# A window-attention, MLP and channel-attention kernel: MLP and channel attention put into one program

## What is computed

```python
# block 0: windows of 8 x 8 shifted by 4, attention over 12 heads, then an MLP over channels
xn = _layernorm(x, norm1_g, norm1_b)
attn = softmax(q @ k.T * scale + bias + mask)
x = shortcut + roll(attn @ v @ proj_w + proj_b)
h = _layernorm(x, norm2_g, norm2_b)
h = gelu(h @ fc1_w + fc1_b)
x = x + (h @ fc2_w + fc2_b)
# block 1: channel attention; mean and variance are of a whole image
mu = mean(x, axis=(1, 2, 3)); var = mean((x - mu) ** 2, axis=(1, 2, 3))
xn = (x - mu) * rsqrt(var + EPS) * ln_g + ln_b
Q, K, V = (_proj(xn, ...) for q, k, v)     # 12 x 12 product per head, then a depthwise 3 x 3 convolution
attn = softmax(K.T @ Q / alpha)            # per head, 12 x 12
out = w_f @ (V @ attn) + b_f + xn
```

## Time and profile before

| | |
|---|---|
| median of 3 runs | 541.57 us |
| the 3 runs | 533.67, 541.57, 545.07 us |
| span of the profiled execution | 540.4 us (the page gives no time of its own for it) |
| PE busy | 518.1 us, 96% |
| VectorE, ScalarE, GpSimd busy | 365.9, 302.1, 178.3 us |
| DMA | 32.51 MB, 60 GB/s |
| window attention | 0 to 263 us |
| MLP, PE's part | 263.7 to 349.4 us |
| first convolution of the channel attention | 378.24 us |

### The profile page before, as it was taken

One profiled execution on the slowest core, in us unless ns is written; L12 is line 12 of the kernel. 1 busy time (PEld: TensorE's weight loads), 2 busy tenths in 40 slices (PEclk: granted clock), 3 DMA queues, 4 the chain that ended last, 5 costly groups with the idle time before them and its releaser, 6 DMA issues. The chain is left out here.

```text
span 540.4 us, 23612 instructions
## 1 busy us (share of the span) xinstructions
PE 518.1 (96%) x9134; PEld 343.1 (63%) x9134; DVE 365.9 (68%) x1003; ACT 302.1 (56%) x763; POOL 178.3 (33%) x216
## 2 busy tenths in 40 slices
PE   7999999999999999998899999939999999999996
PEld 6777777777777777776674343339655655555553
DVE  1479999999999999997404354436556565656544
ACT  2278877777787778876435563103444444444432
POOL 8433444444434443344200220022433332333300
PEclk8599999999999999999999999957999999999999
DMA  4111111111111101100130132323454434444411
GB/s 83 29 42 32 30 30 46 29 30 30 30 29 24 26 24 29 29 3 2 45 75 21 46 93 71 88 49 79 121 146 124 115 101 118 121 114 105 117 51 32
DMA packets 41177, 32.51 MB, mean 60 GB/s; under 512 B 19240, under 2 KB 36776, under 8 KB 41128
## 3 DMA queue, kind: packets, MB, share of 16 engines
q1 hardware_dynamic: 37544, 26.11, 18.9%
q0 software_dynamic: 3584, 5.72, 4.8%
HBM read 18.36 MB, written 7.13 MB: 47 GB/s over the span
## 5 line engine op out<-in xcount | busy, mean ns | idle before, releaser
L383 POOL TENSOR_TENSOR scores<-scores,peak 128x768 f32<-128x768 f32 x64 | 94.3, 1473 | 135.3 <-DVE peak L552 135.3
L1224 POOL DMA_DIRECT2D x_stack<-padded_x x96 | 52.4, 548 | 97.4 <-PE ps_v L1497 63.4
L446 ACT COPY probs_t<-ps_probs 128x768 f32<-128x768 f32 x64 | 51.1, 799 | 40.7 <-PE ps_probs L706 40.7
L544 DVE TENSOR_TENSOR scores<-ps_scores,bias 128x768 f32<-128x768 f32 x64 | 61.3, 957 | 9.1 <-PE ps_scores L696 7.4
L552 DVE TENSOR_REDUCE peak<-scores 128x12 f32<-128x768 f32 x64 | 61.0, 953 | 2.4
L719 PE MATMUL ps_out<-v_blocks,probs_t 128*64 128x54 f32 x1536 | 57.2, 224 | 1.0 <-ACT out_t L451 0.9
L719 PEld LDWEIGHTS ps_out<-v_blocks,probs_t 128*64 128x64 f32 x1536 | 50.2, 138 | 12.3 <-issue 12.2
L706 PE MATMUL ps_probs<-ident,scores 128*128 128x128 f32 x384 | 55.0, 279 | 0.0
L440 ACT ACTIVATE scores<-scores 128x768 f32<-128x768 f32 x64 | 54.2, 846 | 0.6 <-POOL scores L383 0.6
L1037 ACT ACTIVATE hidden<-ps_hidden,fc_b_folded 128x512 f32<-128x512 f32 x48 | 29.1, 688 | 36.8 <-PE ps_hidden L978 36.8
L1497 PE MATMUL ps_qk<-x_stack,conv_w 40*32 40x256 f32 x1536 | 48.8, 379 | 0.0
(11 more groups left out here) (156 smaller groups left out, 900.2 us busy)
## 6 DMA issues: line engine op xcount, KB each, us to landing
x_stack<-padded_x SPq DMA_DIRECT2D x96, 54.0 KB
x_stack<-padded_x POOLq DMA_DIRECT2D x96, 54.0 KB, 2.7
padded_x<-x_pad SPq DMA_DIRECT2D x32, 121.5 KB, 2.5
x_sliced<-stream SPq DMA_DIRECT2D x48, 64.0 KB, 2.0
mixed<-y_sliced SPq DMA_DIRECT2D x48, 64.0 KB, 2.0
out<-y_sb SPq DMA_DIRECT2D x32, 96.0 KB, 2.0
x_now<-in_x SPq DMA_DIRECT2D x32, 72.0 KB, 1.8
stream<-in_x SPq DMA_DIRECT2D x32, 72.0 KB, 1.9
```

Of the source, the lines that this page charges most:

```text
L383: nc.gpsimd.tensor_tensor(sc, sc, peak[:, par, p, :].unsqueeze(2).to_broadcast((128, HEADS, WN)), ALU.subtract).then_inc(s["shifted"], 1)
L446: nc.scalar.copy(probs_t[:, :], ps_turned).then_inc(s["turned_copied"], 1)
L544: nc.vector.tensor_tensor(scores[:, par, p, :].rearrange("p (g c) -> p g c", g=NG), ps_scores[:, :, 0:GROUP * WN], bias[:, p, :].rearrange ...
L1224: engine.dma_start(x_stack[64 * half + i * HC:64 * half + (i + 1) * HC, slot, :, :], rows).then_inc(landed[slot], 16)
```

## The change

`mlp` and `channel_attention` become one function, `mlp_and_channel_attention`, in one block with no meeting of the engines between them, and all fills in both are gone. The parts:

- Banks: `ps_hidden` (4), `ps_y` (2) and `ps_turn` (2) serve both halves; each bank of the channel attention is one of these. `mixed` is now the same memory as `stream`, so `join_y` also waits until the tokens of its group were turned and its residual input was read.
- The second up-product of group 0 goes to `ps_y` and `ps_turn` (`hidden_home`); it waits for no Gelu, and the third waits for the first Gelu alone.
- Weight products are made at the start of the MLP on DVE, turned by PE in group 0 in `ps_y`, and copied to `conv_w` by DVE in place of ACT.
- Inverse deviations of groups 2 and 3 are made on POOL, by an addition and a power (`token_deviation_by_power`), and ACT loads no table for them. Those of the images are powers on POOL too.
- The moments of an image are dealt with in two batches of 16. Batch 0 (groups 0 and 1) is summed in the last group; images 0 to 5 are normalised there, and ACT pads them and issues their writes itself. Batch 1 is summed in the loop at images 5 and 6, and the moments of the last group are taken in the loop behind images 1 to 4.
- SP gathers images 0 to 3 ahead of the last group's 12 writes.
- `down(g, 0)` waits for the Gelu of each part by itself. The straight part ahead of the loop has 8 images in place of 4.

The names `s["..._3"]` of the channel attention are now `s3[...]`. The diff, cut:

```diff
-                fill(nc, ps_y[0:C, 0, 0:C], average[:, :], 26)
...
-                fill(nc, ps_y[0:C, 0, 0:C], average[:, :], 26)
...
-                fill(nc, ps_y[0:C, 0, 0:C], average[:, :], 6)
...
+def token_deviation_by_power(nc, pool, m, s, g, exponent, shifted):
+    pool.wait_ge(s["spread_ready"], (g + 1) * QUARTERS * BLOCKS)
+    need(pool, s["scaled_ready"], g * QUARTERS)
+    need(pool, shifted, (g - 2))
+    nc.gpsimd.tensor_scalar(m["log_var2"][:, :, :], m["spread_mlp"][:, :, :, 1], EPS, None, ALU.add).then_inc(shifted, 1)
+    pool.wait_ge(shifted, g - 1)
+    nc.gpsimd.tensor_tensor(m["rstd2"][:, :, :], m["log_var2"][:, :, :],
+                            exponent[:, 0:1].unsqueeze(2).to_broadcast((128, QUARTERS, BLOCKS)),
+                            ALU.pow).then_inc(s["rstd_ready"], 1)
...
+def lap_loop(engine, step, between=None):
+    for t in range(LEAD_LAPS * SLOTS):
+        step(t, t // SLOTS, t % SLOTS)
+    if between:
+        between()
+    with engine.Fori(LEAD_LAPS, B // SLOTS - 2) as i:
         for slot in range(SLOTS):
             step(i * SLOTS + slot, i, slot)
     for t in range(B - 2 * SLOTS, B):
         step(t, t // SLOTS, t % SLOTS)
...
+    mixed = stream
...
+    ps_weights = [ps_y[:, bank_of, 0:SIDE * C].rearrange("p (j c) -> p j c", j=SIDE) for bank_of in (1, 0, 1)]
+    ps_final = ps_y[:, 1, SIDE * C:SIDE * C + C]
+    ps_v, ps_qk = ps_hidden[:, 0:ROUNDS, 0:N], ps_turn[:, 0:ROUNDS, 0:N]
+    ps_tok = ps_hidden[:, 2, :].rearrange("p (n r c) -> p n r c", n=2, r=ROUNDS)
+    ps_gram = ps_hidden[:, 3, 0:ROUNDS * HC].rearrange("p (r d) -> p r d", r=ROUNDS)
+    ps_av, ps_final_y = ps_y[:, 0, 0:N], ps_y[0:C, 1, 0:N]
+    ps_moments = {0: ps_turn[0:C, 0, 0:2 * EARLY], 1: ps_hidden[0:C, 2, 0:2 * EARLY]}
...
+    def hidden_home(g, part, r):
+        if g == 0 and part == 1:
+            return ps_y[:, r, :] if r < 2 else ps_turn[:, r - 2, :]
+        return ps_hidden[:, r, :]
...
+        slice_x(0)
+        slice_x(1)
...
+        for g in range(LAST):
+            for c in range(SLICES):
+                join_y(g, c)
+            if g + 2 < GROUPS:
+                slice_x(g + 2)
+        for t in range(SLOTS):
+            gather(sp, t, 0, t, 0, stacked_sp)
+        for c in range(SLICES):
+            join_y(LAST, c)
...
+        for g in range(2, GROUPS):
+            token_deviation_by_power(nc, pool, m, s, g, exponent, variance_shifted)
+            for r in range(QUARTERS):
+                scale_tokens(nc, pool, m, s, g, r)
+        def take_inverse_roots(batch):
+            own = slice(batch * EARLY, (batch + 1) * EARLY)
+            pool.wait_ge(moments_set, (batch + 1) * MOMENT_STEPS)
+            nc.gpsimd.tensor_tensor(moments[:, own, 0], spread2[:, :, 1], exponent[0:C, 0:1].to_broadcast((C, EARLY)),
+                                    ALU.pow).then_inc(deviations_set, 1)
+        take_inverse_roots(0)
...
+        def start_image(t):
+            pad_x(t, t // SLOTS, t % SLOTS)
+            write_padded(act, t, t % SLOTS)
...
+            gelu(g, 1)
+            if later:
+                for r in range(2, QUARTERS):
+                    copy_tokens(nc, act, m, s, (g + 1) * QUARTERS + r, tokens_home(r))
+            if g == LAST:
+                act.wait_ge(cleared, CLEARED)
+                start_image(0)
+                start_image(1)
+            gelu(g, 2)
...
+        for t in range(2, AHEAD):
+            start_image(t)
...
+        def center_means(batch):
+            own = slice(batch * EARLY, (batch + 1) * EARLY)
+            done = batch * MOMENT_STEPS
+            sums = ps_moments[batch].rearrange("p (t e) -> p t e", e=2)
+            dve.wait_ge(means_summed, batch + 1)
+            need(dve, deviations_set, batch)
+            nc.vector.tensor_reduce(mean_sum[:, :], sums, AX_X, ALU.add).then_inc(moments_set, 1)
+            dve.wait_ge(moments_set, done + 1)
+            nc.vector.scalar_tensor_tensor(out=off_mean[:, :, :], in0=mean_sum[:, :].unsqueeze(2).to_broadcast((C, EARLY, 2)),
+                                           scalar=-0.5, in1=stats[:, own, 1::3], op0=ALU.mult, op1=ALU.add).then_inc(moments_set, 1)
+            nc.vector.tensor_scalar(moments[:, own, 1], mean_sum[:, :], -0.5, None, ALU.mult).then_inc(moments_set, 1)
+            dve.wait_ge(moments_set, done + 2)
+            nc.vector.scalar_tensor_tensor(out=spread2[:, :, :], in0=off_mean[:, :, :], scalar=0.5, in1=off_mean[:, :, :],
+                                           op0=ALU.mult, op1=ALU.mult).then_inc(moments_set, 1)
+            dve.wait_ge(moments_set, done + 4)
+            nc.vector.scalar_tensor_tensor(out=spread2[:, :, :], in0=stats[:, own, 2::3], scalar=1.0 / N, in1=spread2[:, :, :],
+                                           op0=ALU.mult, op1=ALU.add).then_inc(moments_set, 1)
...
+            dve.wait_ge(spreads_summed, batch + 1)
+            nc.vector.tensor_reduce(spread2[:, :, 0], sums, AX_X, ALU.add).then_inc(moments_set, 1)
+            dve.wait_ge(moments_set, done + 6)
+            nc.vector.tensor_scalar(spread2[:, :, 1], spread2[:, :, 0], EPS, None, ALU.add).then_inc(moments_set, 1)
...
+            if isinstance(t, int) and t < AHEAD:
+                dve.wait_ge(deviations_set, 1)
+                shift = moments[:, t, 1:2]
+            else:
+                dve.wait_ge(s3["moment_ready"], t - AHEAD + 1)
+                shift = moment[:, par, 1:2]
...
+        make_products()
...
+            if g > 0:
+                add_residual(g - 1, 0)
+            if last:
+                center_means(0)
...
+            if last:
+                take_deviations(0)
+                normalise_image(0)
+                normalise_image(1)
+            if more:
+                for c in range(SLICES):
+                    copy_normed(g + 1, c)
+            if g == 0:
+                for place, kind in enumerate((1, 0, 2)):
+                    copy_weights(place, kind)
+                copy_final()
+            if g > 0:
+                add_residual(g - 1, 2)
...
+        normalise_image(2)
+        normalise_image(3)
+        add_residual(LAST, 0)
+        normalise_image(4)
+        normalise_image(5)
+        add_residual(LAST, 1)
+        take_moments(LAST - 1, 0, 4)
+        add_residual(LAST, 2)
+        take_moments(LAST - 1, 4, 8)
...
+            if is_image(t, STATS_LATE + 1):
+                center_means(1)
+            if is_image(t, STATS_LATE + 2):
+                take_deviations(1)
...
+            if isinstance(t, int) and 1 <= t <= STATS_LATE:
+                take_moments(LAST, 2 * (t - 1), 2 * t)
...
+            if g > 0 or part == 2:
+                need(pe, s["gelu_ready"], (g * HT + part) * QUARTERS if g > 0 else QUARTERS)
...
+                pe.wait_ge(weights_copied, 2 * ROUNDS)
+            if n == 1:
+                pe.wait_ge(weights_copied, 3 * ROUNDS + 1)
+            need(pe, s["mixed_ready"], (n - 1) * 2)
+            for h in range(HT):
+                if c == 0:
+                    pe.wait_ge(s["gelu_ready"], (g * HT + h + 1) * QUARTERS)
...
+        def turn_weights(place, kind):
+            pe.wait_ge(products_set, 3 * ROUNDS * (place + 1))
+            need(pe, weights_copied, ROUNDS * (place - 1))
...
+            if last:
+                sum_means(0)
...
+            if last:
+                sum_spreads(0)
...
+            if g == 0:
+                turn_back(1, 0)
+                turn_back(1, 1)
+                turn_weights(0, 1)
+                turn_weights(1, 0)
+                turn_back(1, 2)
+                turn_weights(2, 2)
+                nc.tensor.transpose(ps_final, w["final"][:, :], ident[0:C, 0:C]).then_inc(weights_turned, 1)
+            elif more:
+                for c in range(SLICES):
+                    turn_back(g + 1, c)
+        for c in range(SLICES):
+            down(LAST, c)
+        pe.wait_ge(ones_in, 16 * ROUNDS)
+        pe.wait_ge(cleared, CLEARED)
         def convolve(t, slot, kind, ps, ready):
```

722 lines of the change are left out of this document (324 added, 398 removed).

## The result

| | before | after |
|---|---|---|
| time, four executions each, same chip | 542.02 us median (533.67 to 545.07) | 518.79 us median (512.89 to 522.25) |
| ratio after / before | | 0.9643, 95% interval 0.9576 to 0.971 |
| profiled execution: time, span | span 540.4 | 512.89 us, span 511.1 |

The kernel is faster by 3.6%. The forecast was 511.4 us with a range of 503 to 521; the ratio puts the changed kernel at 0.9643 x 541.57 = 522.2 us, just above the range, while the median itself, 518.79, lies inside it and 7.4 above the forecast. The executions of both kernels fall into two clusters some 6 to 8 us apart, with three of each kernel's four in the upper one, and within a cluster the kernels differ by 21 to 23 us, not by the forecast's 30.

A forecast was written before the change was run, and what follows sets the result against it. PE was taken to set the end throughout, waiting for image 0 between 349.4 and 378.2. Terms -7.6 - 24.1 + 1.5 = -30.2 us on a span of 540.4 gave 510.2, carried over to 511.4 us, range 503 to 521.

The forecast's parts named there:

- group 0: First MLP group: fills removed and up-products run back to back, 13.1 us in place of 20.7, a gain of 7.6.
- groups 1 and 2: Middle MLP groups: inverse deviations move to POOL, new instructions hidden under PE's work, no gain or loss.
- last group and hand-over: Last group's first up-product to first convolution: +29.0 us where it was +53.1, a gain of 24.1.
- loop: Image loop after the first convolution: added moments and small operations partly hidden, +1.5 us, bounds 0.3 and 4.
- With 16 elements per partition against 768 I take 0.5, inside the cover: Groups 1 and 2: POOL's new addition and power taken at 0.5 us, inside a cover of 2.0, costing nothing.
- rival B: POOL's power is dear: 2.4 us in each of two groups, 1.8 in image 0's chain, about 518; chance 0.13.
- rival A: Clock falls to 1.2 GHz at the last group's new wait, costing 2 to 5 us, about 515; chance 0.20.
- the new wait: Last group: PE waits 2.8 us for group 1's moments before summing the means of the first 16 images.
- three signs of being wrong: Clock at 1.2 GHz after 323, a POOL power over 1 us, or the first convolution waiting for a DMA.
- the allowance of 0.9 for gaps: Last group: first convolution worked out at +28.1 us, taken as +29.0 with gaps.
- C: SP's queue falls 7 us further back, image 4's gather comes late, loop waits once, about 519; chance 0.06.
- D: Slower: clock falls at the new wait and stays at 1.2 GHz through the loop, 556 us; chance 0.01.

The follow-up runs named there:

- r0: The kernel after once more, unchanged, six executions beside the kernel before: 512.12 us, ratio 0.9482.
- b1: Kernel after with group 0's second up-product back in the same banks as the first, no fills: 528.23 us.
- b2: Kernel after with group 0 as in the kernel before, same banks and the old fills: 528.79 us.
- d1: Kernel before without the three fill calls of the MLP's group 0: 542.55 us.
- a1: Kernel after with the inverse deviations of groups 2 and 3 back on ScalarE, with table loads: 520.98 us.
- a2: Kernel after with the inverse deviations of images 0 to 15 made on ScalarE instead of by a GpSimd power: 518.45 us.
- a5: Kernel after with the power of images 0 to 15 in two parts, images 0 to 5 first: 509.98 us.
- c2: Kernel after with a3, a5 and a1 together, six executions: 505.09 us, ratio 0.9383 to before.
- a3: Kernel after with the sum of means one up-product later and the sum of spreads one down-product later: 511.04 us.
- a4: Kernel after with 26 fills ahead of the sum of the means in the last group: 512.22 us.
- e1: Kernel after with the convolution's weights turned and copied behind the last down-product, two `ps_y` banks swapped: 531.06 us.
- e2: Kernel after with images 0 to 15's statistics, and images 0 to 5's normalising and padding, behind the last group; SP writes before gathers: 533.71 us.

## Why the prediction was wrong

It gave 30.2 us between the two kernels. The traces give 23.6, and the measured medians 23.2. In the later six executions, r0, the interval of the ratio (0.9396 to 0.9567) contains the forecast's 0.944, but the trace among them gives 22.8, with nearly the same stages as after's. The account below is of these stages.

| term | forecast | measured | tested by |
|---|---|---|---|
| group 0 | -7.6 | -8.5 | b1, b2, d1 |
| groups 1 and 2 | 0 | +2.1 | a1 |
| last group and hand-over | -24.1 | -18.9 | a2 to a5, c2 |
| loop | +1.5 | +1.6 | |
| sum (measured, from unrounded terms) | -30.2 | -23.6 | |

**The step that failed most is "With 16 elements per partition against 768 I take 0.5, inside the cover".** The power takes 2.9 us, and the 2.18 that I took as the most for one instruction did not hold it either: I bounded an operation that no row showed by the dearest row of another kind, a product. The cover of 2.0 us that I worked out for group 2 was right: 2.93 + 0.26 stands 1.2 over it, and 1.4 was lost there and 0.7 in group 1. In the hand-over the same instruction is 2.5 us longer than my 0.4, and the wait for the last Gelu was 2.5 us instead of 0.3 (a2 and a5 tie the one to the other). Together some 4.3 us. That was rival B, at a chance of 0.13 and inside its price of 6.6. The late first call of 6 us that rival B also named did not come: the first power, at 282.98, stands straight behind its addition and takes 2.94.

**The second is the weighing of rival A.** "What follows here is dense" was my reason against it, and the clock fell all the same, at the new wait and again at the Gelu's, for 1.7 us each: 3.4 us (a3, a4 and the 6.21 against 7.91). Its price lay in my range of 2 to 5, at a chance of 0.20. My rival list treated A and B as one or the other; they came together, since B makes the second wait at which A strikes. The path that the forecast walked was right, through the down-products and not through `x_stack`, and the two prices that add to it were each counted alone. Two of the three signs of being wrong that it named came: 1.2 GHz after 323 (0.50 from 324 to 326) and a power of over 1 us. The Trainium skill (TensorE: Matmul & The Clock Gate, "HAM oscillation — how this bites in real kernels") has waits between bursts bring the next burst back at the low clock; the prediction set this aside for the short gaps of the MLP, and the rows of after and b1 behind waits of 2.5 and 3.2 us agree with the page; behind a3's 2.22 and a5's 1.44 the clock stayed.

The rest balances: the new wait came 0.45 us later than worked out (+0.45), the allowance of 0.9 for gaps was not needed (-0.9), group 0 was 0.9 better, the loop 0.1 worse. 4.3 + 3.4 + 0.45 - 0.9 - 0.9 + 0.1 = 6.5, of a miss of 6.6.

**Group 0: right, for a reason half seen.** The walk (three products to 8.2, 1.42 of wait for VectorE's copy, 12.2 in all) comes out at the lower bound, but not on its condition: the copies were not hidden, and what was saved is the allowance of 0.4, 0.3 on the three products, and the small transposes at about 0.1 instead of 0.14 each. That the clock held behind the wait for the copy, also in after, was luck: in r0, a1, a2 and e2 it did not, for 1.7 us more in group 1. I counted the removed fills as pure loss; b1, b2 and d1 show that they gave back some 3.4 of their 5.3 us by keeping the clock up, and could go at full gain only because the waits under them went.

**Groups 1 and 2's own products, the loop, rivals C and D: right.** The loop lost 1.6. Image 4's gathering held nothing up, or the loop would have lost more. D's mechanism is real, as e1 and e2 show (10 us in the loop), but not in after, where the loop runs at 2.4 GHz: its first convolution follows the last down-product without a wait.

**What stays open.** The 13.2 us between before's 53.0 and e2's 39.8 I have not taken apart: in it are the weights, the fills and the wait for the last group's own moments. The weights cost 1.9 us in group 0 (b2) and 3.3 behind the last product (e1); what they cost among before's fills no run shows. Open too is why the clock falls behind the same wait in one trace and not in another: behind the 1.42 us in group 0, behind the two gaps near 246 us, and in b2's loop.

## What to carry to other kernels

Where a change puts an operation on an engine for which no row has a price, measure one of it by itself first, at two sizes, before a cover is held against it: neither its element count nor another operation's row bounds it. A new wait of TensorE can cost its length and a slow product behind it, as the waits of 2.5 and 3.2 us did here, so count both, and look first for a later place for the waiting instruction (6.5 us here) rather than a filler (0.5). Fills that look like waste beside a wait may give back much of what they cost (3.4 of 5.3 us here); the larger gain lies in removing the wait. And before a slow product is put down to an edit, see whether it runs ahead of what the edit touches, as the first one of b1 and d1 does.

## What the runs showed of the hardware

- A power on GpSimd takes 2.93 us for 128 x 16, 2.90 for 96 x 16, 1.95 for 96 x 10 and 1.32 for 96 x 6: paid by the element of a partition, and not by the partitions. Four scalings of 128 x 384 take 3.18.
- A table load on ScalarE took 1.28 us in the traces read here, and the activation behind it began at its end (315.65 + 1.28, Gelu at 316.94 in a1). The Trainium skill (ScalarE: Activation LUTs, "What ACT_TABLE_LOAD costs") gives about 1.28 us for the load and 1.38 for a drain, 2.66 together for every switch. The trace agrees with the first and shows nothing of the second; by an estimate from the page's whole figure a1's deviations would come 1.4 us later and the turn-back, which just meets the scalings, would wait as long, and group 2 took 20.41.
- The granted clock after a stand still differs widely. After waits of 3.19 and 2.51 us it was at 1.2 GHz for about 3.4 us each time; after a wait of 2.22 in a3 it did not fall; after one of 1.42 in group 0 it fell in 4 of 11 traces; after 3.3 us of thin work in e1 and 13.4 us of none in e2 it stayed at 1.2 GHz through 24 us of unbroken products. In before's hand-over it had risen after 10 us of fills.
- Even small gaps may do it: near 246 us of the window attention (251.5 in before), code that is the same in all kernels, PE waits 0.9 and 0.6 us. In 7 of the 14 traces (a1, a2, a3, b1, d1, e1, e2) the clock falls there and returns only after 10 to 14 us; in the other 7 (before, after, r0, a4, a5, b2, c2) it stays. No run takes the gaps away, so that they are the cause is not shown. Among the runs of after and its variants the MLP starts at 261.5 to 264.7 us where it falls and at 256.9 to 258.1 where it stays, whatever the kernel does behind it, which is why stages and not spans are compared here.
